# Products nobody reads, added on TensorE in the fold ahead of a gated recurrence and butterfly FFN kernel

## What is computed

```
x = x + layernorm(x) * r
h = layernorm(x) @ W_exp + b_exp              # 512 -> 2048
h = butterfly(h, up_weights)                   # 11 stages of 2x2 blocks
h = gelu(h + up_bias)
h = butterfly(h, down_weights)                 # 11 stages
x = x + h @ W_con + b_con + down_bias          # 2048 -> 512
```

## Time and profile before

| | |
|---|---|
| median of 3 runs | 2770.97 us (2770.18 to 2772.96) |
| profiled execution, its own time | 2771.06 us |
| its span, first to last instruction | 2769.2 us |
| TensorE busy | 2740.1 us, 99% |
| VectorE busy | 2122.9 us, 77% |
| ScalarE busy | 1131.0 us, 41% |
| GpSimd busy | 396.5 us, 14% |
| mean granted clock of TensorE | 0.995 |

### The profile page before, as it was taken

The page is one execution under the profiler, slowest core; times in us unless marked ns, Lnnn a source line. Parts: engine busy times, 40 slices in busy tenths (PEclk is TensorE's granted clock), DMA queues, the critical chain, the costliest instruction groups (busy, mean ns, idle before and its releaser), DMA issues.

```text
span 2769.2 us, 35072 instructions
## 1 busy us (share of the span) xinstructions
PE 2740.1 (99%) x12191; PEld 2260.4 (82%) x12191; DVE 2122.9 (77%) x3554; ACT 1131.0 (41%) x1715; POOL 396.5 (14%) x561
## 2 busy tenths in 40 slices
PE   8899999999999999999999999999999999999998
PEld 6778888888888888888888888888888888888887
DVE  9878787778878777787877878787787877778533
ACT  5743434334343433434343343434434343343432
POOL 4712011110201111010110101011020111102000
PEclk8999999999999999999999999999999999999999
DMA  9795765758576575856757585675857557584543
GB/s 275 266 294 152 216 191 167 228 154 240 165 204 203 168 213 155 255 163 195 201 170 223 155 239 168 190 214 162 235 152 224 185 175 223 161 243 152 182 149 99
DMA packets 292021, 540.48 MB, mean 195 GB/s; under 512 B 36918, under 2 KB 98518, under 8 KB 274950
## 3 DMA queue, kind: packets, MB, share of 16 engines
q1 hardware_dynamic: 285456, 535.77, 64.7%
q10 hardware_dynamic: 5414, 1.25, 0.3%
q0 software_dynamic: 976, 1.22, 0.2%
HBM read 445.83 MB, written 60.82 MB: 183 GB/s over the span
## 4 chain that ended last, share of the span: by engine, by line
PE 98%; ACT 1%; issue 0%; DVE 0%; DMA 0%; ACTq 0%
PE ps L1767 44%; PE ps L1788 25%; PE ps L1801 25%; PE ps L1664 1%; PE ps L1570 1%; PE ps L1642 0%; PE ps L1668 0%; ACT wcon L863 0%; PE ps L1662 0%; ACT w1r L885 0%; PE ps L1670 0%; PE ps L1868 0%; DMA wexp<-in_L_ffn_W_exp_dram 0%; PE ps L1716 0%; PE ps L1589 0%
## 5 line engine op out<-in xcount | busy, mean ns | idle before, releaser
L1767 PE MATMUL ps<-xop,w1r 128*128 128x512 f32 x5376 | 1364.1, 389 | 2.5 <-DVE xop L1296 1.6
L1767 PEld LDWEIGHTS ps<-xop,w1r 128*128 128x128 f32 x5376 | 1008.8, 188 | 212.7 <-DVE xop L1296 2.0
L1788 PE MATMUL ps<-w2r,ghi 128*128 128x512 f32 x2048 | 630.5, 389 | 0.0
L1801 PE MATMUL ps<-w2r,ghi 128*128 128x512 f32 x2032 | 625.8, 389 | 0.0
L1002 ACT ACTIVATE st<-ps 128x512 f32<-128x512 f32 x384 | 229.7, 598 | 839.9 <-PE ps L1767 839.9
L1403 DVE TENSOR_TENSOR x<-ps,x 128x512 f32<-128x512 f32 x508 | 348.6, 686 | 280.6 <-PE ps L1801 278.2
L1788 PEld LDWEIGHTS ps<-w2r,ghi 128*128 128x128 f32 x2048 | 384.4, 188 | 79.8
L1801 PEld LDWEIGHTS ps<-w2r,ghi 128*128 128x128 f32 x2032 | 381.2, 188 | 79.8 <-DVE glo L1426 0.4
L1421 DVE TENSOR_TENSOR g<-ps,st 128x512 f32<-128x512 f32 x384 | 262.9, 685 | 212.5 <-PE ps L1767 212.1
L1006 ACT ACTIVATE g<-g,gelu_bias 128x512 f32<-128x512 f32 x384 | 275.4, 717 | 362.7 <-DVE g L1421 361.6
L1426 DVE TENSOR_TENSOR glo<-g,ghi 128x512 fp32r<-128x512 f32 x510 | 347.5, 702 | 79.9 <-ACT ghi L1020 79.8
(11 more groups left out here) (174 smaller groups left out, 1701.8 us busy)
## 6 DMA issues: line engine op xcount, KB each, us to landing
w1r<-w_products SPq DMA_DIRECT2D x889, 256.0 KB, 3.3
w2r<-w_split SPq DMA_DIRECT2D x126, 1024.0 KB, 5.0
x<-in_x_dram SPq DMA_DIRECT2D x128, 256.0 KB, 7.2
raw<-kv SPq DMA_DIRECT2D x480, 64.0 KB, 2.2
out_dram<-x SPq DMA_DIRECT2D x120, 256.0 KB, 4.0
kv<-in_ctx_dram SPq DMA_DIRECT2D x64, 256.0 KB, 7.3
raw<-in_ctx_dram SPq DMA_DIRECT2D x64, 256.0 KB, 5.3
wexp<-in_L_ffn_W_exp_dram SPq DMA_DIRECT2D x4, 1024.0 KB, 10.9
```

Of the source, the lines that this page charges most:

```text
L1767: last = nc.tensor.matmul(bank[:, :], w1r[:, slot, w, c * P:(c + 1) * P], xop[:, XPOS[m], v, c, :], start=(opens and i == 0), stop=(i == l ...
L1788: last = nc.tensor.matmul(ps_ya[j][:, :], g[:, p % 2, q, j * P:(j + 1) * P], w2r[:, p % 2, kk, w, :], start=(p == 0 and kk == 0 and i == 0 ...
L1801: last = nc.tensor.matmul(ps_yb[:, :], g[:, p % 2, q, j * P:(j + 1) * P], w2r[:, p % 2, kk, w, :], start=(kk == 0 and i == 0), stop=(kk == ...
```

## The change

Two things are added to TensorE's list and nothing is taken away. Behind the wait for `ident`, ahead of the first `WT` step, the unit matrix is transposed 32 times into bank `ps_f[0]`. And a new function `keep_clock` issues products of the first selection matrix with all 512 columns of `sel_parts` into the bank that `high_up` 0 will use, waiting for the same count as that step. It is called six times with four products, between groups of spreads behind the low fold; to make room for the calls, the high spreads are cut in two and two and the downward low ones in whole and plain. The order of the spreads among themselves stays. No result of the added products is read.

```diff
+            def keep_clock(kind, i, products):
+                n = fold_at(kind, i)
+                who, count = kept_count[n - 3]
+                pe.wait_ge(fold_kept[who], count)
+                for _ in range(products):
+                    nc.tensor.matmul(ps_f[n % 3][:, :], sel_parts[:, 0, 0, :],
+                                     sel_parts[:, :, :, :].rearrange("p s b m -> p (s b m)"), start=True, stop=True)
+
             spread_low, spread_high, spread_top = spread(0)
             spread_low_dn, spread_high_dn, spread_top_dn = spread(1)
+            for _ in range(32):
+                nc.tensor.transpose(ps_f[0][:, 0:P], ident[:, :], ident[:, :])
             for k in range(KH):
                 if k == KH // 2:
                     spread_low(range(LOWS))
@@
             for k in range(KH):
                 wait_kept(pe, "WT", k)
                 fold_step("low_up", k)
-            spread_high(range(HIGH))
-            spread_low_dn(range(PARTED[0]))
-            spread_high_dn(range(HIGH))
+            spread_high(range(2))
+            keep_clock("high_up", 0, 4)
+            spread_high(range(2, HIGH))
+            keep_clock("high_up", 0, 4)
+            spread_low_dn(WHOLE)
+            keep_clock("high_up", 0, 4)
+            spread_low_dn(PLAIN)
+            keep_clock("high_up", 0, 4)
+            spread_high_dn(range(2))
+            keep_clock("high_up", 0, 4)
+            spread_high_dn(range(2, HIGH))
+            keep_clock("high_up", 0, 4)
             pe.wait_ge(high_matrix_ready, 1)
```

## The result

The kernel with the added products takes 2780.72 us in the median of six runs (2780.05 to 2783.17), against 2771.34 us before (six runs, 2770.18 to 2772.96): ratio 1.0035, 95% interval 1.0024 to 1.0046. That is 9.4 us slower where I forecast 0.4, and outside my range. The profiled execution took 2782.13 us, with a span of 2780.3.

The account below looks back on a forecast made before the run. TensorE bounds the kernel, its main loop untouched and half clock ahead of it the target; opening -0.9 plus wide products +1.3 (5.5 paid, 4.2 given back) made +0.4 us on 2771.06, so 2771.5 us, range 2768.0 to 2776.0.

Parts of the forecast that it names:

- the products hold the clock: Between low and high fold, 24 wide products keep TensorE at full clock from 45.8 to 59.5 us; net +1.3 us.
- rival (2): Spreads behind the low fold: too few wide products, clock falls as before, nothing given back; 2781.6 us, chance 0.05.
- the third fall: Half clock up to 84:88 us, near the bias products; left as is, its start may move, some 2 us either way.
- The price of a wide product: Between the spread groups: 0.23 us each at full clock, 24 products cost 5.5 us.
- My upper bound: Wide products between the spreads: 24 x 0.48 us at half clock with nothing given back, +11.4 us.
- What could be given back: Low to high fold at full clock: high spreads 1.35, whole 0.7, plain 0.8, high fold's products 1.4; sum 4.2 us.
- the narrow spreads are poor at using the clock: Spreads between the folds: held by weight loads for few columns, so 13.7 us at half clock gives back 4.2, not 6.8.
- The opening: Start of TensorE's list: 32 added transposes raise the clock before the real ones; -0.9 us, ends -2.0 and +0.5.
- From there VectorE's chain of subtractions, casts and path products reaches the low fold: From 16.54 us VectorE runs through 28.0 us almost without a gap; its subtraction can start at least 0.55 us earlier.
- VectorE's stall behind GpSimd's fill: Opening: VectorE's 3.17 us cast ends with GpSimd's fill at 13.5 us; an earlier cast might slip ahead, counted as nothing.
- rival (1): Opening: the transposes never raise the clock, all behind ScalarE moves about 2.5 us; 2774.9 us, chance 0.05.
- The cover and the pass-through: High matrix (54.3 us at worst) and folded rows (56.4) precede the high fold; TensorE waits for nobody, shifts reach the main loop.

Follow-up runs that it names:

- the last experiment: Kernel before, nothing added, the two broad downward high spreads moved behind the high fold's steps 1 and 2: 2773.57 us against 2770.92, ratio 1.0011.

## Why the prediction was wrong

**The step that failed** is the one that the products hold the clock. I gave my rival (2) 0.05, "the wide products are too few, the clock falls as before", and it is what happens. I had named the argument for it (the spreads between the groups are what lowered the clock) and set against it that wide products at half clock fill twice the time. They do, and it is not enough: 24 us at one half in the change, 23.9 us with the wide products alone, and with twelve in a place it still fell several times. Rival (2) put the time at 2781.6 us, close to the 2780.7 measured, and partly by luck. In the two profiles the main loop comes 11.3 us late, made of three parts: the low fold 1.6 us late, 11.9 in the stretch, and 2.2 won back where the third fall stayed away. Rival (2) had 11.4 for the stretch and -0.9 for the opening.

**The price of a wide product** was mis-sized too. I took 0.23 us from six of them in a row. Between narrow spreads a group of four takes 1.14 us at full clock, so even with the clock held it would be 6 x 1.14 = 6.8 us and not 5.5. In the change it was 11.1. My upper bound, 0.48 each with nothing given back, was the right end at 11.4.

**What could be given back** came near in its sum and not in its parts. At full clock the whole spreads take 1.51 instead of 2.55 us (1.0, I had 0.7), the two narrowest high ones 1.23 (the upward ones) instead of 2.10 (the downward ones of the run with 24 products alone), so 0.9, but the plain ones 3.00 instead of 3.07 and the broad high ones 2.89 instead of 3.00 (0.1 each, where I had 0.8 for the plain ones alone). The first 32 records of the high fold take 3.57 instead of 5.14 (1.6, I had 1.4). That is 3.7 us in all, so by this sum the change would have lost 3.1 us even if its purpose had been met; no run held the clock with these products. The prediction's sentence that the narrow spreads are poor at using the clock is wrong for the narrowest (2.74 us at half clock throughout, 1.51 at full) and right only for the broad ones.

**The opening**: -0.9 us forecast, +0.6 measured with an interval on both sides of nothing. The transposes were free, as said, the first real ones started at 6.8 to 8.2 us and ran quickly. The step that failed is "From there VectorE's chain of subtractions, casts and path products reaches the low fold". ScalarE and VectorE did come earlier (16.24 instead of 16.54 us, in the changed kernel by 0.7 us at the first copy), but the low fold does not hang on them. It hangs on TensorE's own rows from the first spread on, and the wait of 0.35 us for line 1603 in the earlier trace rows had shown it. The first spread starts at 14.14 us in before and after alike, because VectorE's stall behind GpSimd's fill did not go: in the run with the transposes alone the cast started 0.2 us earlier (10.41 against 10.63) and was caught.

In the run with the transposes alone nothing but transposes ran before, and sixteen real ones took 1.95 us instead of 3.4 to 3.7, so rival (1) is out. The Trainium skill ("TensorE: Matmul & The Clock Gate", Part 4) has it that transposes do not bring the full clock. Here they did.

**The cover and the pass-through** held in the main. TensorE waited for nobody at the start of the high fold, though the 56.4 us for the folded rows were too late a reading, as the last experiment shows. Of the 13.5 us that it came late, 11.3 reached the main loop; the rest is the third fall, which did not take place, as I had left open ("some 2 us either way").

## What to carry to other kernels

Before adding work to hold a clock, add up what the slow stretch could give back at most, kind by kind, and hold it against the price of the fill where it will stand, between other instructions and not in a row of its own: here 3.7 against 6.8 us. Do not guess from the width of a product what the clock is worth to it: the spreads of 16 columns nearly halved, those of 128 and 256 did not change. And follow a gain on one engine to the place where two engines meet, and look who waits for whom there: a wait of 0.35 us at the end of VectorE's chain said that TensorE comes last, and nothing won on VectorE ahead of it could count.

## What the runs showed of the hardware

Moments of the clock drift between executions of one program: the first fall lay between 14.4 and 18.3 us in the profiles, with the transposes or without, and the same kernel (two sparse f32 products in each place) was at half clock for 6.8 us of the stretch's falls in one execution and 23.9 in another, a difference of 6 us in time. A single profile, or a single pair, does not show what a change does to the clock.

Eight records of broad f32 spreads (128 and 256 columns, 16 and 8 rows) took 2.9 to 3.1 us at either clock. Eight of 32 and 64 columns went from 2.10 us at half to 1.23 at full clock, twelve of 16 columns from 2.74 to 1.51. It was the broader ones that gained nothing, which I had not expected and have no cause for.
